# Top-2 expert layer: three batches sorted by expert on the chip, the last one dense

## The reference

```python
x = x + attn(layernorm(x), W_qkv, b_qkv, W_o, b_o)             # 16 heads of 64, own RMS norm, causal, softmax over queries
x = x + xattn(layernorm(x), ctx, ctx, Wq, ..., bo)             # 16 heads of 8
x = x + ffn(layernorm(x), Wr, br, W1, b1, W2, b2)
def ffn(x, ...):                                              # K = 2, E = 8, D = 128, H = 512
    scores = einsum('bsd,de->bse', x, Wr) + br
    _, topk_idx = top_k(scores, K)
    indicator = one_hot(topk_idx, E).sum(-2)
    weights = softmax(where(indicator > 0, scores, -inf))
    for i in range(E):
        xi = x * indicator[..., i:i+1]
        h = relu(einsum('bsd,dh->bsh', xi, W1[i]) + b1[i])
        yi = einsum('bsh,hd->bsd', h, W2[i]) + b2[i]
        out = out + yi * weights[..., i:i+1]
```

## Time and profile before

| | us |
|---|---|
| median of three runs | 324.4 |
| the profiled execution | 326.34 |
| its span, first to last instruction | 324.6 |
| PE busy | 297.8 |
| DVE busy | 206.5 |
| ACT busy | 193.0 |
| POOL busy | 97.8 |

### The profile page before, as it was taken

How to read it: one execution, slowest core, us unless ns; L and a number is a source line. 1 busy time by engine, 2 the same in 40 slices (tenths; PEclk the granted TensorE clock), 3 DMA queues, 4 the chain that set the end, 5 groups by cost and what they waited for, 6 DMA issues and landing times.

```text
span 324.6 us, 5407 instructions
## 1 busy us (share of the span) xinstructions
PE 297.8 (92%) x1869; PEld 210.2 (65%) x1869; DVE 206.5 (64%) x444; ACT 193.0 (59%) x525; POOL 97.8 (30%) x140
## 2 busy tenths in 40 slices
PE   6789999999989899797989788889999999999995
PEld 2578677877777568453745343436778878678883
DVE  3767657375548885966376673536686867666652
ACT  1569858387747664466276668867655465354451
POOL 7990190035020200720056152055558110000000
PEclk9799999999999999999999999979999999999999
DMA  8900015530100010001084491000000000100001
GB/s 234 210 3 3 1 23 65 67 43 16 36 0 2 16 35 2 5 0 45 5 253 141 112 280 55 3 0 2 0 1 2 0 0 0 35 0 0 2 1 32
DMA packets 14889, 14.06 MB, mean 43 GB/s; under 512 B 2620, under 2 KB 10892, under 8 KB 14860
## 3 DMA queue, kind: packets, MB, share of 16 engines
q1 hardware_dynamic: 13278, 12.92, 16.4%
q10 hardware_dynamic: 1584, 0.80, 0.9%
HBM read 9.94 MB, written 0.52 MB: 32 GB/s over the span
## 4 chain that ended last, share of the span: by engine, by line
PE 73%; DVE 13%; ACT 3%; DMA 3%; issue 3%; SPq 2%; POOL 1%; DVEq 0%; ACTq 0%; POOLq 0%
PE ps L663 7%; PE ps L665 7%; PE ps L664 7%; PE ps L737 6%; PE ps L770 5%; PE ps L782 4%; PE ps L944 4%; PE ps L945 4%; PE ps L946 4%; DVE mneg L1306 4%; PE ps L815 3%; PE ps L852 3%; PE ps L744 2%; SPq L412 2%; DMA w_in<-in_L_attn_W_qkv 2%
## 5 line engine op out<-in xcount | busy, mean ns | idle before, releaser
L1062 ACT ACTIVATE p<-ps,negmax 128x256 f32<-128x256 f32 (+1 forms) x128 | 52.7, 426 | 25.2 <-DVE negmax L1277 24.7
L1392 DVE SCALAR_TENSOR_TENSOR hid_lo<-ps,hid_hi 128x512 fp32r<-128x512 f32 x64 | 43.6, 688 | 33.7 <-ACT hid_hi L1126 33.4
L1306 DVE TENSOR_REDUCE mneg<-ps 128x2 f32<-128x512 f32 x64 | 42.5, 684 | 18.6 <-PE ps L815 18.5
L1126 ACT ACTIVATE hid_hi<-ps 128x512 fp32r<-128x512 f32 x64 | 37.5, 598 | 26.8 <-PE ps L665 26.7
L1092 ACT ACTIVATE px<-ps 128x512 f32<-128x512 f32 x64 | 36.1, 598 | 17.8 <-PE ps L837 17.5
L1277 DVE TENSOR_REDUCE negmax<-ps 128x2 f32<-128x512 f32 (+1 forms) x48 | 32.9, 686 | 19.6 <-PE ps L739 12.5
L815 PE MATMUL ps<-k_st,q_mem 128*128 128x256 bf16 x128 | 24.7, 276 | 9.0 <-DVE mneg L1306 7.6
L504 POOL TENSOR_SCALAR tmp<-mv 128x2 f32<-128x2 f32 x8 | 1.9, 233 | 95.3 <-DVE mv L1301 95.3
L1048 ACT CAST t_hi<-ps 128x512 fp32r<-128x512 f32 x32 | 18.8, 592 | 19.5 <-PE ps L665 18.6
L663 PE MATMUL ps<-x_hi,w_hi 128*128 128x512 f32 x64 | 25.6, 400 | 1.7 <-issue 1.5
L1062 ACT ACTIVATION_READ_ACCUMULATOR p<-ps,negmax 128x1 f32 x128 | 26.6, 208 | 0.0
(11 more groups left out here) (184 smaller groups left out, 663.7 us busy)
## 6 DMA issues: line engine op xcount, KB each, us to landing
w_raw<-in_L_ffn_W SPq DMA_DIRECT2D x2, 1024.0 KB, 6.1
w_last<-in_L_ffn_W SPq DMA_DIRECT2D x8, 256.0 KB, 6.1
k_st<-k_part SPq DMA_DIRECT2D x12, 128.0 KB
q_mem<-q_part SPq DMA_DIRECT2D x48, 32.0 KB
w_in<-in_L_attn_W_qkv ACTq DMA_DIRECT2D x2, 384.0 KB, 6.3
w_in<-in_L_attn_W_qkv SPq DMA_DIRECT2D x2, 384.0 KB, 7.1
resid<-in_x SPq DMA_DIRECT2D x2, 256.0 KB, 4.0
p<-in_L_attn_W_o SPq DMA_DIRECT2D x1, 512.0 KB, 8.3
```

The costliest lines, as they stand in the source:

```text
L1062: last = act.activation(dst, bank[:, n * i:n * i + n], ACT.Exp, bias=negmax[:, kt, h:h + 1], accum_out=psums[:, kt, h:h + 1])
L1126: act.activation(hid[0][:, c, :], ps[:, hidden_banks[NC * k + c], :], ACT.Relu).then_inc(s_ha, 1)
L1306: dve.tensor_reduce(mneg[:, qt, :].rearrange("p (r g) -> p r g", r=2)[:, :, g], ps[:, max_bank[("MX", b, u)], :].rearrange("p (h k) -> p h ...
L1392: dve.scalar_tensor_tensor(hid[1][:, c, :], ps[:, hidden_banks[NC * k + c], :], 0.0, hid[0][:, c, :].bitcast(F32), ALU.max, ALU.subtract). ...
```

## The change

Batches 0 to 2 (six tiles of 128 tokens, 1536 token-expert pairs) are sorted: each pair gets a row in one of 13 tiles of `CAP` = 256 rows, one tile for each expert and 5 spare ones for an expert's pairs beyond 256. Batch 3 stays dense. So the expert layer is now a sequence `SEQ` of 13 sorted tiles and 8 dense ones (batch 3 by each expert), all of 256 columns. Its steps:

- `ranks` (`PS`, PE) counts, with nine products for batches 0 and 1 and six for batch 2, how many pairs of the same expert stand ahead of a pair; `places` (DVE, twelve dependent steps until the row numbers stand) turns that into a row number. Batches 0 and 1 are group 0, batch 2 is group 1 (`ROUTED`). The choice of the two best stands in (3, 0) for group 0, its places in (3, 2); for group 1 they are in (3, 5) and (3, 6.5).
- `dispatch` (POOL) writes the normalised rows of one tile for one of its two experts to a DRAM buffer `xs` with an indirect DMA: 12 of them, 8 for group 0 and 4 for group 1. SP then reads `xs` back in three parts, after all 12 have landed.
- `rows_in` (PE) transposes the rows of two tiles to `X_BANK`; `rows_high`, `rows_low` split them straight from PSUM. `hidden` and `combine` work in units of two 128-feature pieces: 6 products of 256 columns for a unit, 24 for a tile.
- `tile_out` (ACT) adds the second bias, `YT` turns the tile back (PE), `rows_out` (DVE) copies it out, `collect` (POOL) writes it with two indirect DMAs to `ys`, 26 in all. SP reads `ys` back for each batch, and `add_pairs` (`CB`, DVE, 8 instructions for a batch) adds the two weighted rows to the residual, in the 7th and 8th dense tile.
- The weights of a spare tile are found at run time (`spares`, `OV`) and copied by SP from SBUF to SBUF, four DMAs of 256 KB for a tile, after all `second_weights` are done.
- All output steps of batch 2 stand in slots (3, 0.5) to (3, 2.5) now; all of the cross-attention is done ahead of the first expert tile; the output steps of batch 3 stand in tiles 0 and 1.
- POOL's order is in the diff. `NT` of group 0 waits for `norm_3(1)`, `NT` of group 1 in slot (3, 4) waits for `norm_3(2)`.

```diff
-LAST_RING = 3
+LAST_HALF = NE // 2
+DT, ST = TPB, NT - TPB
+PAIRS = 2 * ST * P
+CAP = 256
+SPARE = PAIRS // (CAP + 1)
+NS = NE + SPARE
+SEQ = tuple([("S", j) for j in range(NS)] + [("D", e) for e in range(NE)])
+ROUTED = ((0, 2 * TPB), (2 * TPB, ST), (ST, NT))
...
-            more = {(1, 6): [("WS", 0, 0)], (2, 1): [("WS", 0, 1)], (2, 5): [("WS", 0, 2)], (2, 6): [("NT", 0)],
-                    (2, 7): [("RT", 0)], (3, 0): [("EX", 0)], (3, 0.5): [("GT", 0)], (3, 2): [("W2", 0, 0)],
-                    (3, 3): [("WT", 0), ("WS", 0, 3)], (3, 4): [("X", 0)]}
+            more = {(1, 4): [("WS", 0, 0)], (1, 5): [("WS", 0, 1)], (1, 6): [("WS", 0, 2)],
+                    (1, 7): [("WS", 0, 3), ("BT", 0)], (2, 0): [("WS", 0, 4)], (2, 1): [("WS", 0, 5)],
+                    (2, 2): [("WS", 0, 6)], (2, 3): [("WS", 0, 7)], (2, 4): [("XC", 0)], (2, 5): [("W2", 0, 0)],
+                    (2, 7): [("W2", 0, 1)], (3, -0.5): [("NT", 0)], (3, 0): [("RT", 0), ("XC", 1)],
+                    (3, 1): [("W2", 0, 2)], (3, 2): [("PS", 0)], (3, 3): [("W2", 0, 3)], (3, 4): [("NT", 1)],
+                    (3, 5): [("RT", 1), ("XC", 2)], (3, 6): [("W2", 0, 4)], (3, 6.5): [("PS", 1)]}
...
+        slots.append([("CO", last, 3), ("W2", 0, 5), ("W2", 0, 6), ("OV", 0)])
+        beside = {(0, 0, "h"): [("oq0", last)], (0, 1, "h"): [("oq1", last), ("W2", 0, 7)], (1, 0, "y"): [("oT0", last)],
+                  (1, 0, "h"): [("oT1", last)], (1, 1, "y"): [("wo", last)], (2, 1, "h"): [("NT", 2)], (3, 0, "y"): [("RT", 2)],
...
+                  (NS + 6, 0, "h"): [("CB", 0)], (NS + 6, 1, "h"): [("CB", 1)], (NS + 7, 0, "h"): [("CB", 2)]}
...
+            sp.wait_ge(s_xs, 16 * 2 * ST)
+            for i, (n0, n1) in enumerate(XR_PARTS):
+                sp.dma_start(xr[:, 2 * n0:2 * n1, :], xs.rearrange("(n p) d -> p n d", p=P)[:, 2 * n0:2 * n1, :]
+                             ).then_inc(s_xr[i], 16)
...
+            for i in range(4):
+                second_weights(i)
+            pool.wait_ge(s_init, 16)
+            for t in range(ROUTED[0][1]):
+                for c in range(2):
+                    dispatch(t, c)
             norm_3(2)
-            first_low(3)
-            second_weights(1)
-            second_weights(2)
+            for t in range(*ROUTED[1]):
+                for c in range(2):
+                    dispatch(t, c)
+            second_weights(4)
+            second_weights(5)
             norm_3(3)
-            for i in range(4, NE):
-                first_low(i)
-                second_weights(i - 1)
-            second_weights(NE - 1)
+            second_weights(6)
+            second_weights(7)
+            for j in range(NS):
+                collect(j)
...
+            def dispatch(t, c):
+
+                pool.wait_ge(s_pos, 1 if t < ROUTED[0][1] else 2)
+                pool.wait_ge(s_n3, t + 1) if c == 0 else pool.wait_ge(s_copied, t // TPB + 1)
+                pool.indirect_dma_start(xs, bass.IndirectOffsetOnAxis(pos_i[:, t, c:c + 1], 0),
+                                        xrow[:, t, c, :], None).then_inc(s_xs, 16)
...
+            def rows_out(j):
+                dve.wait_ge(s_misc, misc_at[("YT", j)] + 1)
+                ge(dve, s_ys[j % 2], 32 * (j // 2))
+                dve.tensor_copy(yrow[:, j % 2, :], ps[:, 7, 0:CAP]).then_inc(s_misc_ev, 1)
```

More of the change, by code:

```diff
@@ L290, in decoder_layer @@
                 slot += maxima_now[1:2] + turn + (tail.get(g, []) if b else []) + maxima_now[2:] + more.get((b, g), [])
[L291 to L312, removed]
+                slots.append(slot)
@@ new lines, in decoder_layer @@
+        y_done = {}
+        for i in range(len(SEQ) + 1):
+            slot = [("X", x) for x, tiles in enumerate(x_units) if x == i == 0 or x and tiles[0] == i + 1]
+            for u in range(2):
+                if i:
+                    slot += [("Y", i - 1, u)]
+                    kind, j = SEQ[i - 1]
+                    if u == 1 and kind == "S":
+                        slot += [("E", j)]
+                    if u == 0 and i >= 2 and SEQ[i - 2][0] == "S":
+                        slot += [("YT", SEQ[i - 2][1])]
+                slot += beside.get((i, u, "y"), [])
+                if i < len(SEQ):
+                    slot += [("H", i, u)]
+                slot += beside.get((i, u, "h"), [])
+            if i == NS + 2:
+                slot += [("B2", 0)]
@@ L313, in decoder_layer @@
             slots.append(slot)
-        slots.append([("YE", 1, 0), ("YE", 1, 1), ("YO", 1, 0), ("YO", 1, 1)])
-        MISC = ("PJ", "n2T", "q", "mT", "oq0", "oT0", "oq1", "oT1", "wo", "NT", "RT", "WT", "YO")
+        slots.append([("YD", 0), ("YO", 0)])
+        MISC = ("PJ", "n2T", "q", "mT", "oq0", "oT0", "oq1", "oT1", "wo", "NT", "RT", "WT", "BT", "YT", "YO")
         misc_at = {k: i for i, k in enumerate(k for slot in slots for k in slot if k[0] in MISC)}
-        X_BANK = 6
-        def turn_bank(hf, i):
-            return X_BANK if (hf, i) == (1, 1) else 7
+        X_BANK, R_BANK = 6, 5
@@ new lines, in ranks @@
+                pe.matmul(count, below[:, :], one[:, :, :], start=True, stop=False)
+                if g == 1:
+                    pe.wait_ge(s_hot, 2)
+                    pe.matmul(count, ones[:, :], seen[:, :].unsqueeze(1).to_broadcast([P, n + 1, NE]), start=False, stop=False)
+                for j in range(n):
+                    last = pe.matmul(count[:, j + 1:n + 1, :], ones[:, :], one[:, j:j + 1, :].to_broadcast([P, n - j, NE]),
+                                     start=False, stop=(j == n - 1))
@@ L948, in second_bias @@
-            def second_bias(hf):
-                pe.wait_ge(s_b2, 32)
-                pe.matmul(ps[:, Y_BANK[hf], :], b2_sb[:, :], wgtT[:, 512 * hf:512 * hf + 512].bitcast(F32),
-                          start=False, stop=False)
+                    pe.wait_ge(s_rank_ev, 2)
+                for n in range(2):
+                    c = slice(P * (2 * u + n), P * (2 * u + n) + P)
+                    if kind == "D" or j < NE:
+                        w = [w[:, j, c] for w in w1_p]
+                    else:
+                        w = [ovw[:, j % 2, k, c] for k in range(2)]
+                    last = products(ps[:, bank, CAP * n:CAP * n + CAP], w,
+                                    [part[:, x % 2, CAP * half_x:CAP * half_x + CAP] for part in x_p])
@@ new lines, in add_pairs @@
+            def add_pairs(b):
+                dve.wait_ge(s_yg[b], 16)
+                dve.wait_ge(s_n3, TPB * (b + 1))
+                for c in range(2):
+                    for t in range(TPB * b, TPB * b + TPB):
+                        dve.scalar_tensor_tensor(resid[:, t, :], yg[:, 2 * t + c, :], gate[:, 2 + c, t:t + 1],
+                                                 resid[:, t, :], ALU.mult, ALU.add).then_inc(s_sum, 1)
+                    dve.wait_ge(s_sum, 2 * TPB * b + TPB * (c + 1))
```

616 lines of the change are left out of this document (435 added, 181 removed).

## The result

| | before | after |
|---|---|---|
| median, us (range) | 324.33 (324.14 to 324.47) | 344.81 (343.61 to 345.21) |
| the profiled execution | 326.34 | 343.61 |
| its span | 324.6 | 341.8 |
| first hidden product | 214.64 | 249.82 |
| last `combine` | 319.93 | 337.86 |

The ratio is 1.0626, with a 95% interval from 1.0598 to 1.0654: slower by 20 us, against a forecast of 337.0. That is inside the stated range of 320 to 351, and 0.8 us above the narrower band, 329 to 344, that the prediction called its forecast. From the first hidden product to the end of the span it is 18.0 us less (110.0 before, 92.0 after), and that product is 35.2 us later. By the prediction's own count some 4.5 of the 18.0 are cross-attention of batch 3, which has only moved to the front.

A forecast was written before the change was run, and what follows sets the result against it. PE's pace was taken to bound the expert layer. First hidden product 246.8 + 74.7 to the last combine + 3.5 + 3.2 + 3.2 + 1.5 = 332.9, plus 4.3: span 337.2, median forecast 337.0; range 320 to 351.

The forecast's parts named there:

- ACT's extra work delays batch 3 by 1.8 us: From 176 to 204, ACT gets 4.1 us more work; batch 3's slots begin 1.8 us later, at 205.7 (bounds 0 and 4.1).
- POOL's queue holds the first dispatch until 219: Ahead of the first dispatch: row numbers at 218.9, POOL's weight pieces through second_weights(3) end at 219.0, then it starts.
- A dispatch takes 0.9 us: Each indirect DMA on POOL takes 0.9 us (bounds 0.2 and 2.0); group 0's eight take 7.2, ending at 226.2.
- Rival B: Dispatches on POOL take 2 us each, by their own work or DVE holding the port: +13.2, 350 us; chance 0.14.
- Nine idle us at `NT(1)`, nine before the rows: PE waits about 9 us at NT(1) for norm_3(2), then idles 9 us before the first hidden product at 246.8.
- Dense pairs 3.5 us: In dense tiles, gated, high and rest parts delay the next rest part about 1 us for each of four pairs: 3.5.
- The fifth tile waits 3.2 us for its weights: At the first spare tile, PE waits 3.2 us for weights copied after second_weights(7), behind norm_3(3) (bounds 0 and 7).
- The pairs' sums 3.2 us: Late in the dense tiles, add_pairs' 24 DVE instructions of 0.23 us and three waits cost 3.2 us (bounds 1 and 6).
- The clock 1.5 us: Behind PE's two longer pauses, the lower granted clock costs 1.5 us (0 to 4).
- 256-column products at 0.12 us in a long run: In the expert layer, 504 products of 256 columns on PE at 0.12 us each take 60.5 us.
- rival C: In the expert layer, 256-column products do not hold 0.12 us; at 0.14 it is +10, 347 us; chance 0.05.
- Rival A: From 205.7 to 246.8, routing is short: first dispatch 6.6 us earlier, dispatches 0.4 each, add_pairs hidden: 321 us; chance 0.18.

The follow-up runs named there:

- the last run above: The kernel with the parts placed anew, with DVE's spare-tile steps moved earlier, norm_3(3) ahead of POOL's last two weight copies, 14 and 6 unread products: 327.07 us, ratio 1.0066.
- the one with the parts placed anew: Changed kernel with batch 0's routing and batch 3's output steps earlier, norm_3(2) behind the sixth dispatch, most weight copies behind the last, dense parts late: 329.03 us, ratio 1.011.
- 3.8 by the experiment: Changed kernel with rows_high and rows_low of a dense pair put behind the next ReLU and rest part: 342.19 us, ratio 1.051.
- by the experiment 4.9: Changed kernel with POOL making second_weights(6) and (7) ahead of norm_3(3) instead of after it: 340.56 us, ratio 1.0476.
- the run with 62 and 44: Changed kernel with 62 unread 512-column products on PE before NT(1) and 44 before the first row transposes: 342.58 us, ratio 1.0498.

## Why the prediction came out as it did

The direction and the mechanism were right: the row trip bounds the front, `norm_3(2)` stands behind eight dispatches, and the expert layer's gain doesn't pay for it. The median is 7.8 us above the forecast. Of these, 4.6 are the span. The other 3.2 come from turning a span into a median: each run is about 1.8 us longer than its span, but the profiled execution of the kernel before was 2.0 us above its median, and that of the changed kernel 1.2 below. By the prediction's steps:

1. *ACT's extra work delays batch 3 by 1.8 us.* No: ACT was busy for 21.98 us in the stretch, and still batch 3's first exp came at 202.81, 1.1 us earlier than before and not 1.8 later. The first dispatch came at 217.66, 1.3 us before the forecast. `oT0` waited 2.2 us for DVE's division, as said.
2. *POOL's queue holds the first dispatch until 219.* Right in time, by luck as to the cause. `second_weights(3)` ended at 216.76 and the row numbers came at 216.80, since the last step of `places(0)` took 0.87 us, until that copy ended (0.17 for the same step without a copy beside it, in the last run above). The dispatch followed the row numbers by 0.86 us. In the last run and the one with the parts placed anew it followed them by 0.86 to 0.87 too, though POOL had been idle for over 7 us. So the row numbers release the first dispatch, and POOL's copy cost 0.7 us by holding DVE, not by its place in the queue.
3. *A dispatch takes 0.9 us.* The first mis-sized term: 0.96 and 0.30 between two, 1.26. Twelve make 4.3 us more, 2.9 of them in the first eight. Rival B (2 us) is out: but for the first of all (1.24) and the first behind `norm_3(2)` (1.10) each took 0.95 to 0.97, in the last run above too, where DVE had its steps for the spare tiles beside two of them (from 230.29 to 232.75, the dispatches at 230.65 and 231.92).
4. *Nine idle us at `NT(1)`, nine before the rows.* Measured 14.4 and 10.1. PE was at `NT(1)` by 216.0, not 219.5. From `NT(1)` to the second group's first dispatch 7.65, forecast 7.7; landing and way back 5.2 with the issue, forecast 4.8 and 0.9 for the last dispatch. The first hidden product: 249.8 against 246.8, which is 1.3 less for the start of the dispatches and 4.3 more for their length.
5. *Dense pairs 3.5 us.* Measured 1.01 + 1.02 + 0.57 + 0.92 = 3.5, and 3.8 by the experiment.
6. *The fifth tile waits 3.2 us for its weights.* Measured 3.38; by the experiment 4.9 with the slow clock behind it.
7. *The pairs' sums 3.2 us.* Mis-sized. They are 4 instructions of 0.31 us a batch, 12 in all, not 24 as the text before the result says, and PE waited 0.45 us for the first two sums and up to 0.7 for the third: 1.2.
8. *The clock 1.5 us.* The second mis-sized term: 4.3 by the experiment with products that nobody reads, just above the upper bound of 4; 1.3 of it come through step 6.
9. *256-column products at 0.12 us in a long run.* Right at the full clock; starts are 0.12 apart (265.83 and 265.95), so rival C is out. At the lower clock they are 0.21 apart (272.67 and 272.88).

From the first hidden product to the end of the last `combine` (338.1) 88.3 us were measured and 86.1 forecast: 2.8 more for the clock, 2.0 less for the sums, 0.2 more at the fifth tile. That leaves 1.2, or 2.5 if the 1.3 us that clock and fifth tile share are counted once, and no experiment assigns them to a place. Behind the last `combine` it is 0.6 less than forecast, so the 4.6 us of the span are 3.0 + 2.2 - 0.6. That the error is no larger is partly luck: the earlier start and the cheaper sums took back 3.3 of the 7.1 us by which dispatches and clock were too low. Rival A is out by the runs themselves: 321 us would have needed the first dispatch 6.6 us earlier and at 0.4 each, and the last kernel above, with its first dispatch at 211.93, was still not below before.

The trip also explains why none of the orders tried here won. In the kernel with the parts placed anew it is 33.9 us from the first dispatch to the first hidden product (213.40 to 247.28); PE has 15.4 us of work to put there (7.1 in the changed kernel, both in part at the lower clock) and is idle for 18.5, 3.3 of them by DVE's late `x_lo`. Its first hidden product is 32.6 us later than before, and from there to the end it is 28.0 us shorter: the two nearly cancel. That no order can win is not shown; the last kernel ends 0.7% above before, and its own products made its last wait longer.

## What to carry to other kernels

Work that shrinks on the bound engine but needs a trip through DRAM first is worth its saving less whatever part of the trip nothing else can fill: write that trip as a row of issues, landing, reading and the first tile's splits, before looking at the saving. On an in-order queue put what the bound engine waits for ahead of a batch of issues, whatever their order looks like in the algorithm. A pause costs again after it, in the clock; filling it helps only if the filling ends when the data is there.

## What the runs showed of the hardware

- An indirect DMA of 128 rows of 528 bytes held GpSimd for 0.96 us, with 0.30 before the next: 1.26 us from start to start. The first of all held it for 1.24 and the first behind other work of GpSimd for 1.10. The first one started 0.86 to 0.87 us after the row numbers that it waits for, in three runs.
- A VectorE step between SBUF tiles can be held over several GpSimd instructions in a row: 5.51 us for 8 columns, from the second of six copies until the last one ended. It is not one instruction's wait (1.22 us each). The Trainium skill (SBUF — State Buffer, "SBUF: two separate sides") has the shared port as a lock that is held for an instruction; the trace shows a longer wait. In the same stretch `resid`, which reads PSUM, went in 0.42 us.
- After the pauses the granted clock came back late: 0.66 in the 29 us with pauses, then 0.75 over 15 us in which PE was busy for 13.2, and 0.86 over the next 13 with a pause of 3.4 in them. The starts show where: products of 256 columns are 0.21 us apart from 249.8 on and 0.12 apart from 254.9 on. With products in the pauses the clock was 1.00 in the two stretches (the run with 62 and 44).
- Copies of 256 KB from SBUF to SBUF took 2.9 and 3.1 us to land (medians of ten each). The fourth of the first four took 4.47, and these four took 6.5 us from the first issue (265.72) to the last landing (272.24).
